# A two-layer convolution kernel in fp32 on one core: the order in which matmuls write their PSUM banks

## What is computed

```python
# layer 0, for each channel (hx, hy: small sine networks with decay)
k_f = rfft2(outer(hx, hy), s=(512, 512)) / 512
u_f = rfft2(x, s=(512, 512))
x = irfft2(u_f * k_f)[..., :256, :256] + x * bias
# layer 1, for each image and channel
scores = einsum('bpsd,bptd->bpst', x, x) / sqrt(256)
red = sum(scores * weights[None], axis=-1, keepdims=True)
y = x + red
out = (y - mean(y, (0, 2, 3))) * rsqrt(var(y, (0, 2, 3)) + 1e-5) * gamma + beta
```

## Time and profile before

| | |
|---|---|
| median of 3 runs | 969.0 us (968.86 to 970.37) |
| the profiled execution, own time | 968.82 us |
| its span in the trace | 966.9 us |
| PE busy | 944.4 us (98%), 5436 matmul instructions |
| PEld busy | 829.1 us (86%), 5436 weight loads |
| DVE / ACT / POOL busy | 749.8 / 681.3 / 671.5 us |
| share of PE in the chain that ended last | 95% |

### The profile page before, as it was taken

One profiled execution on the slowest core, in us unless ns is written; L12 is line 12 of the kernel. 1 busy time (PEld: TensorE's weight loads), 2 busy tenths in 40 slices (PEclk: granted clock), 3 DMA queues, 4 the chain that ended last, 5 costly groups with the idle time before them and its releaser, 6 DMA issues.

```text
span 966.9 us, 18768 instructions
## 1 busy us (share of the span) xinstructions
PE 944.4 (98%) x5436; PEld 829.1 (86%) x5436; DVE 749.8 (78%) x2335; ACT 681.3 (70%) x1088; POOL 671.5 (69%) x518
## 2 busy tenths in 40 slices
PE   7999999999999999999999999999999999999993
PEld 5888888888888888888888888888888888888882
DVE  2678878878878878878878778788788788788785
ACT  2547777777777777777777777777767767767756
POOL 2767767767767777777777777777777777777750
PEclk9999999999999999999999999999999999999996
DMA  7765877878878887877778877877787787787634
GB/s 217 263 207 181 273 232 258 275 215 267 274 227 258 277 242 243 274 253 235 271 247 238 274 243 246 271 262 224 274 251 235 278 264 230 271 271 226 226 113 174
DMA packets 73294, 235.90 MB, mean 244 GB/s; under 512 B 7232, under 2 KB 24128, under 8 KB 65088
## 3 DMA queue, kind: packets, MB, share of 16 engines
q1 hardware_dynamic: 73280, 235.73, 75.8%
HBM read 168.40 MB, written 67.31 MB: 244 GB/s over the span
## 4 chain that ended last, share of the span: by engine, by line
PE 95%; ACT 2%; DVE 1%; DMA 1%; POOL 0%; issue 0%; ACTq 0%; DVEq 0%
PE ps_c L483 36%; PE ps_u L483 31%; PE ps_z L483 27%; PE ps_avg L483 1%; ACT out_sb L458 1%; DMA toep_whole<-filters_padded 1%; ACT z_sb L458 0%; DVE z_sb L678 0%; DMA par<-params_in 0%; POOL zl L391 0%; DVE products L700 0%; ACT zh L467 0%; DVE zl L689 0%; DMA filters_padded<-z_sb 0%; DVE z_sb L611 0%
## 5 line engine op out<-in xcount | busy, mean ns | idle before, releaser
L391 POOL TENSOR_TENSOR zl<-z_sb,zh 128x1024 fp32r<-128x1024 f32 x126 | 301.7, 2394 | 207.9 <-ACT zh L467 207.9
L700 DVE CUSTOM_DVE_ANT_0 products<-z_sb,ps_c 128x256 bf16<-128x256 f32 x508 | 183.6, 418 | 158.3 <-PE ps_c L483 158.3
L483 PE MATMUL ps_z<-uh,toep 128*128 128x512 f32 x768 | 270.8, 407 | 0.1
L437 ACT ACTIVATE uh<-ps_u 128x1024 fp32r<-128x1024 f32 x127 | 130.4, 1027 | 197.4 <-PE ps_u L483 197.4
L458 ACT ACTIVATE out_sb<-z_sb,shift,gain 128x256 f32<-128x256 f32 x496 | 257.1, 592 | 6.6
L483 PE MATMUL ps_u<-toep,xh 128*128 128x256 f32 x1016 | 240.0, 317 | 2.3 <-POOL toep L369 2.2
L483 PE MATMUL ps_c<-zh,wh 128*128 128x512 f32 x508 | 197.9, 389 | 1.2 <-DVE zl L689 0.7
L483 PE MATMUL ps_c<-zh,wl 128*128 128x512 f32 x508 | 198.1, 390 | 0.0
L483 PE MATMUL ps_c<-zl,wh 128*128 128x512 f32 x508 | 197.7, 389 | 0.0
L483 PE MATMUL ps_u<-toep_whole,xt_sb 128*128 128x128 f32 x1016 | 195.0, 273 | 0.0
L711 DVE BATCH_NORM_STATS2 stat<-z_sb 128x6 f32<-128x256 f32 x512 | 179.3, 413 | 0.0
(11 more groups left out here) (63 smaller groups left out, 924.9 us busy)
## 6 DMA issues: line engine op xcount, KB each, us to landing
xt_sb<-xt_in SPq DMA_DIRECT2D x64, 1024.0 KB, 9.3
x_sb<-x_in SPq DMA_DIRECT2D x128, 512.0 KB, 7.2
out<-out_sb SPq DMA_DIRECT2D x124, 512.0 KB, 3.5
w_sb<-wt_in SPq DMA_DIRECT2D x64, 256.0 KB, 6.7
toep_whole<-filters_padded SPq DMA_DIRECT2D x64, 256.0 KB, 6.5
out<-z_sb SPq DMA_DIRECT2D x4, 512.0 KB, 3.0
par<-params_in SPq DMA_DIRECT2D x1, 224.0 KB, 4.6
par<-params_in SPq DMA_DIRECT2D x1, 194.0 KB, 2.6
```

What stands on the lines that cost most here:

```text
L391: nc.gpsimd.tensor_tensor(zl[:, zs.slot(2)], z_sb[:, r, h], zh[:, zs.slot(2)].bitcast(F32), ALU.subtract)\
L437: nc.scalar.activation(uh[:, us.slot(2)], u_bank(us)[:, :, :, :], ACT.Copy)\
L483: return nc.tensor.matmul(o, a, b, start=start, stop=stop)
L700: last = nc.vector.tensor_tensor_reduce(products[:, cs.slot(2), k, b], z_sb[:, r, h, k, b], bank[:, k, b], 1.0 / math.sqrt(SIDE), 0.0, ALU ...
```

## The change

The order of the matmuls within each product. Which products are computed, with which operands and shapes, into which places, what is waited for ahead of a product, and which semaphore its last matmul increments stay as they are. Every accumulation group of a bank still ends before the next group of that bank begins.

```diff
@@ product_y (z)
-                for a in range(BLOCKS):
-                    for h in range(a + 1):
-                        cols = slice(P * (a - h), P * (a - h + 1))
-                        t_h, t_l = toep[:, t, 0, 0, cols], toep[:, t, 0, 1, cols]
-                        mm(ps_z[:, a], t_h, uh[:, s, h], h == 0, False)
-                        mm(ps_z[:, a], t_h, ul[:, s, h], False, False)
-                        last = mm(ps_z[:, a], t_l, uh[:, s, h], False, h == a)
+                t_h = [toep[:, t, 0, 0, P * d:P * (d + 1)] for d in range(BLOCKS)]
+                t_l = [toep[:, t, 0, 1, P * d:P * (d + 1)] for d in range(BLOCKS)]
+                mm(ps_z[:, 1], t_h[1], uh[:, s, 0], True, False)
+                mm(ps_z[:, 0], t_h[0], uh[:, s, 0], True, False)
+                mm(ps_z[:, 1], t_h[0], uh[:, s, 1], False, False)
+                mm(ps_z[:, 0], t_h[0], ul[:, s, 0], False, False)
+                mm(ps_z[:, 1], t_h[0], ul[:, s, 1], False, False)
+                mm(ps_z[:, 0], t_l[0], uh[:, s, 0], False, True)
+                mm(ps_z[:, 1], t_l[0], uh[:, s, 1], False, False)
+                mm(ps_z[:, 1], t_h[1], ul[:, s, 0], False, False)
+                last = mm(ps_z[:, 1], t_l[1], uh[:, s, 0], False, True)
@@ product_c (c)
-                for a in range(BLOCKS):
-                    for k in range(BLOCKS):
-                        w_h, w_l = wh[:, w, k, P * a:P * (a + 1)], wl[:, w, k, P * a:P * (a + 1)]
-                        mm(bank[:, a], w_h, zh[:, s, k], k == 0, False)
-                        mm(bank[:, a], w_h, zl[:, s, k], False, False)
-                        last = mm(bank[:, a], w_l, zh[:, s, k], False, k == BLOCKS - 1)
+                rows = [slice(P * a, P * (a + 1)) for a in range(BLOCKS)]
+                for k in range(BLOCKS):
+                    for a in range(BLOCKS):
+                        mm(bank[:, a], wh[:, w, k, rows[a]], zh[:, s, k], k == 0, False)
+                    for a in range(BLOCKS):
+                        mm(bank[:, a], wh[:, w, k, rows[a]], zl[:, s, k], False, False)
+                    for a in range(BLOCKS):
+                        last = mm(bank[:, a], wl[:, w, k, rows[a]], zh[:, s, k], False, k == BLOCKS - 1)
@@ stage (u)
-                    for h in range(BLOCKS):
-                        rows = slice(P * h, P * (h + 1))
-                        for b in range(PAIR):
-                            o = u_bank(us)[:, h, b, :]
-                            mm(o, xh[:, s, b, rows], toep[:, t, 1, 0, :], True, False)
-                            mm(o, xh[:, s, b, rows], toep[:, t, 1, 1, :], False, False)
-                            mm(o, xl[:, s, b, rows], toep[:, t, 1, 0, :], False, False)
-                            last = mm(o[:, P:SIDE], xt_sb[:, r, PAIR * us.half() + b, 1, rows],
+                    rows = [slice(P * h, P * (h + 1)) for h in range(BLOCKS)]
+                    for b in range(PAIR):
+                        o = u_bank(us)[:, :, b, :]
+                        for h in range(BLOCKS):
+                            mm(o[:, h], xh[:, s, b, rows[h]], toep[:, t, 1, 0, :], True, False)
+                        for h in range(BLOCKS):
+                            mm(o[:, h], xh[:, s, b, rows[h]], toep[:, t, 1, 1, :], False, False)
+                        for h in range(BLOCKS):
+                            mm(o[:, h], xl[:, s, b, rows[h]], toep[:, t, 1, 0, :], False, False)
+                        for h in range(BLOCKS):
+                            last = mm(o[:, h, P:SIDE], xt_sb[:, r, PAIR * us.half() + b, 1, rows[h]],
                                       toep_whole[:, r, 1, 0:P], False, True)
```

## The result

The changed kernel takes 971.27 us (median, 970.29 to 972.07), the kernel before in the same comparison 969.71 us (968.75 to 970.56), 20 runs each. The ratio is 1.0016 with a 95% interval of 1.0009 to 1.0023: slower by 1.6 us, a small loss that is clear of noise. The forecast was 969.0 us and no change.

A forecast was written before the change was run, and what follows sets the result against it. PE, never waiting in steady state, was taken as the bound, 128 steps of matmul-start distances. Changes of 0 for c, z and u against the profiled 968.82 us, 0.2 us below the median, gave 969.0 us, range 965.2 to 972.9.

The forecast's parts named there:

- The argument from the crossings already in c and from the warm-up: c's distances with bank changes match 17 one-bank warm-up distances (0.2265 us each), so changing banks saves nothing.
- Rival A: Consecutive accumulations into one bank cost a turn-around in all products; alternating saves 47 us, giving 922 us; chance 5%.
- the unseen seam of one float32 matmul behind another: In u, twice a step, a float32 matmul follows another with other weights; taken as 0.11 us.
- the four seams together: In u, two float32-to-float32 and two 256-to-256-column seams replace mixed ones each step; change taken as 0.
- Sum: 0 + 0 + 0: Products c, z and u each priced from their own rows, each with no change; forecast 969.0 us.
- The bounds set on these seams: Each of u's four new seams may be off 0.01 us either way: 5.1 us at the ends, 2.6 counted.
- so I take 0: z's distances, 0.003 us each above c's, cause undecided, expected unchanged; ends 3.8 us less or 1.3 us more.
- rival C: Fewer float32 switches, two a step instead of four, save up to 2.6 us, z's part 3.8; 965 to 967; 12%.
- Rival B: Separating u's equal-weight pairs loses 5.1 us, 974 us; with the float32 seam mostly 971 to 974 us; chance 13%.
- Its second half: The other unseen seam in u, two float32 matmuls in a row, also slower; included in the 13%.

The follow-up runs named there:

- e_banks: Kernel before, operands in old order, all three products writing banks in the changed kernel's sequence (output wrong); channel 14.447 us, as before.
- e_c: Kernel before with only product c in the new order; 1.0004 of before (0.9994 to 1.0013), channel 14.447 us.
- e_z: Kernel before with only product z in the new order; 1.0004 of before (0.9994 to 1.0013), channel 14.447 us.
- v_last: Kernel before, but the last of u's four groups has its float32 matmul third instead of last; channel 14.453 us against 14.447.
- v_run4: Kernel before, u per image: row block 0's three 256-column matmuls, row block 1's three, then both float32 ones; 1.0016 of before, channel 14.473 us.
- v_alt2: Kernel before, u alternating banks at every matmul, one 256-column matmul between an image's two float32 ones; 0.9995 of before, channel 14.447 us.
- v_best: Kernel before, u per image: four xh 256-column matmuls, both float32 ones, then two xl ones; 966.67 us, 0.9968 of before, channel 14.400 us.
- v_gap1: Kernel before, u per image with both float32 matmuls ahead of the last xl one, so one 256-column matmul follows them; channel 14.480 us.
- v_run4mid: The same kernel as v_best in an earlier execution, both float32 matmuls of each image ahead of its two xl ones; 966.03 us, channel 14.400 us.
- e_u: Kernel before with only product u in the new order, z and c as before; 1.0016 of before (1.0006 to 1.0025), channel 14.473 us.

## Why the prediction was right or wrong

**The bound was right.** PE's stream of matmul starts sets the time, its waits did not change, and 64 x 0.0265 us accounts for all that was lost. The prediction counted anything within 1.9 us as not to be told from no change; 20 runs of each kernel resolve 0.7 us, and the loss of 1.6 us shows.

**Banks: right.** The argument from the crossings already in c and from the warm-up, that a change of bank is worth nothing, held. With e_banks alternating 29 more neighbours in a step the period did not move by 0.001 us. Rival A fell with it. The rule of the Trainium skill, "Perfetto Trace Analysis", section "Matmul Optimizations", that all banks be leveraged, finds nothing to win inside a product here: with all three products alternating, the channel stays at 14.447 us. Other uses of the banks were not tried.

**Products c and z: right for their own reordering only.** e_c and e_z alone: 0. But the terms of the sum were not 0: z grew by 0.008 us and c by 0.005 in the changed kernel, through u.

**The step that failed: a new order of u was given no effect on z and c.** The prediction took 0.11 us for the unseen seam of one float32 matmul behind another and 0 for the four seams together. The 0.11 us is what the rows of after show, and u is 1.16 us an image as said. What was wrong is the assumption under "Sum: 0 + 0 + 0", that a matmul's cost lies in the distance behind it, so that each product can be priced from its own rows. In this stream an order of u shows in the distances of z, up to ten matmuls later; the seams of u were priced rightly row by row and the step still came out 0.013 us longer, 128 x 0.013 = 1.7 us. The bounds set on these seams (0.01 us each, half counted) were wide enough for it, and so was the range: 971.27 lies within 965.2 to 972.9. That is width and not foresight, for the cost is not in the seams that were bounded. The value inside the bounds was chosen as if the terms were independent, and v_last shows that they are not. A sum of seams cannot give the sign here.

**A sign was in the rows and was passed over.** z's 2.07 us against 9 x 0.2267 = 2.04 was read, and put down as either ACT's read or a tail of the float32 matmuls, "so I take 0". Had the second been taken, the forecast would have been that a change at that seam moves z. That would have named the place, not the direction: rival C expected fewer switches to save, and they cost.

**Rival B: right side, wrong mechanism.** It named 971 to 974 us from pairs with equal weights; v_run4 keeps two such pairs in an image and has the full loss, v_alt2 has none of them and no loss. Its second half, two float32 matmuls in a row in u, is the part that survived, though as a cost in z and not at that seam.

**What stays open.** The runs show that the order of the float32 matmuls in u decides where z enters its sequence of distances, which points to something that is carried from one instruction to the next. What that is, and why a distance of two matmuls lets z begin at the sequence's end and a distance of one near its start, no run shows. The periods of all these kernels differ by whole multiples of 0.0033 us a step (0.003, 0.010, 0.013, 0.017, 0.020, 0.023, 0.027), which has no explanation here either.

## What to carry to other kernels

Where PE is the bound and never waits, measure the period of the steady state from the chain and change one product at a time: the product whose rows get longer need not be the one that was edited. Within one product, alternating PSUM banks between neighbouring matmuls was worth nothing; in this kernel, where short float32 matmuls stand in a stream of `float32r` ones, their order ahead of the next product was worth 0.16% one way and 0.32% the other. Such an order has to be tried, since neither the seams' rows nor the length of the run foretold its sign.

## What the runs showed of the hardware that was not expected

- A plain float32 matmul of 128 columns is two instructions of 0.11 us each, about the 0.12 us of a 256-column `float32r` one, and its effect shows later: in v_best z's nine matmuls take 2.05 us, in before 2.07, in v_gap1 2.09, with z's program the same in all three. Averaged by place, z's distances are pieces of one sequence, entered earlier or later.
- A channel's length is reproducible to about 0.001 us: v_run4mid and v_best, one kernel in two executions, both gave 14.400 us; e_u, v_run4 and the changed kernel, alike but for banks and operands, 14.473 each.
- Once it has settled, the distance in the stream of 512-column `float32r` matmuls is 0.2267 us, whether or not neighbours write one bank or share weights (c in before and in e_c), and also while ACT reads `ps_u` (z in v_best) or DVE reads `ps_u` and `ps_z` (c).
